# The sixteen largest keys of each block ahead of the guess, and four index searches in banks of their own

## What is computed

```python
x = x + einsum('oc,bchw->bohw', W, layernorm_over_channels(x))   # W: 32 Householder steps
t = tokens(x)                                                     # 16 images x 256 pixels = 4096 tokens of 128
xf = layernorm(t)
Sm = softmax(xf @ W_router + b_router)                            # 4096 x 32 experts
G, idx = top_k(Sm.T, 128)                                         # 128 tokens for each expert
up = tokens_of(idx) @ W_up[group] + b_up                          # 8 groups of 4 experts, 341 wide
y.at[idx].add(G * (silu(up) @ W_down + b_down))
out = t + y
```

## Time and profile before

| what | value |
|---|---|
| median of 3 runs | 203.8 us (203.35 to 204.65) |
| profiled execution, its own time | 202.58 us |
| its span, first to last instruction | 200.3 us |
| mean granted TensorE clock | 0.802 |
| busy share PE, weight load, VectorE, ScalarE, POOL | 64%, 42%, 50%, 40%, 54% |
| instructions | 2418 |

### The profile page before, as it was taken

How to read it: one execution, slowest core, us unless ns; L and a number is a source line. 1 busy time by engine, 2 the same in 40 slices (tenths; PEclk the granted TensorE clock), 3 DMA queues, 4 the chain that set the end, 5 groups by cost and what they waited for, 6 DMA issues and landing times.

```text
span 200.3 us, 2418 instructions
## 1 busy us (share of the span) xinstructions
PE 128.4 (64%) x670; PEld 83.7 (42%) x673; DVE 99.3 (50%) x409; ACT 81.0 (40%) x290; POOL 108.4 (54%) x121
## 2 busy tenths in 40 slices
PE   1999965304116341110126899999999659999992
PEld 1558954201005110000003666666777524444592
DVE  2464998974774882102001021194674962973600
ACT  3265999346992772110134455534334000000062
POOL 2028479986351377777744366866878678300000
PEclk9999999855555555555555699999999969999999
DMA  4999999999755252222220113333424334599167
GB/s 108 298 341 302 292 289 201 305 398 264 190 157 159 88 211 70 63 65 67 65 56 19 49 15 38 29 27 27 40 26 39 29 28 38 101 324 382 63 183 236
DMA packets 33710, 28.45 MB, mean 142 GB/s; under 512 B 6848, under 2 KB 27408, under 8 KB 33568
## 3 DMA queue, kind: packets, MB, share of 16 engines
q1 hardware_dynamic: 26785, 21.70, 37.5%
q0 software_dynamic: 5472, 4.48, 15.3%
q10 hardware_dynamic: 1440, 2.13, 3.3%
HBM read 17.61 MB, written 10.68 MB: 141 GB/s over the span
## 4 chain that ended last, share of the span: by engine, by line
PE 48%; DVE 17%; POOL 12%; issue 10%; another core or an unknown queue 9%; DMA 2%; ACT 1%; SPq 0%; POOLq 0%; DVEq 0%
PE PZ L1184 7%; PE PT L1148 7%; PE PM L1148 6%; PE PZ L1162 6%; POOL rs L472 4%; PE PM L1184 3%; PE PT L1184 3%; PE PM L1162 3%; POOL rs L465 3%; PE PT L992 2%; DVE wdn L935 2%; DVE junk L923 2%; PE PT L1137 2%; POOL act L478 2%
## 5 line engine op out<-in xcount | busy, mean ns | idle before, releaser
L511 POOL DMA_INDIRECT acc<-X,idx x27 | 42.0, 1557 | 18.4 <-DVE X L967 8.0
L502 POOL DMA_INDIRECT xg<-token_rows,idx x32 | 30.4, 949 | 16.3 <-DVE idx L920 8.3
L935 DVE TENSOR_SCALAR_CACHE_REDUCE wdn<-wide,slot_token 128x1024 bf16<-128x1024 f16 x20 | 25.0, 1272 | 5.5 <-PE PZ L1184 5.5
L1125 PE MATMUL PZ<-cum,onehot 32*128 32x129 f16 x32 | 6.7, 265 | 31.3 <-DVE idx L920 18.8
L1040 PE MATMUL PZ<-stage_w,X 128*128 128x192 f32 x64 | 14.7, 381 | 6.9 <-DVE act L767 6.5
L1162 PE MATMUL PZ<-wdn,act 128*128 128x128 f32 x132 | 17.4, 277 | 1.1 <-DVE X L967 1.1
L645 ACT ACTIVATE X<-PZ 128x512 f32<-128x512 f32 x4 | 2.4, 597 | 38.3 <-PE PZ L1189 38.3
L1125 PEld LDWEIGHTS PZ<-cum,onehot 32*128 32x128 f16 x32 | 3.0, 99 | 34.9 <-issue 30.8
L1162 PEld LDWEIGHTS PZ<-wdn,act 128*128 128x128 f32 x132 | 16.0, 191 | 2.1 <-DVE X L967 1.4
L967 DVE TENSOR_SCALAR X<-PZ,xg 128x128 f32<-128x128 f32 x22 | 7.6, 349 | 18.6 <-PE PZ L1162 18.6
L620 ACT ACTIVATE junk_a<-PZ,slot_half 128x128 f16<-128x128 f32 x16 | 5.8, 363 | 26.7 <-issue 20.8
(11 more groups left out here) (180 smaller groups left out, 278.3 us busy)
## 6 DMA issues: line engine op xcount, KB each, us to landing
X<-in_x SPq DMA_DIRECT2D x8, 256.0 KB, 5.2
acc<-zero SPq DMA_DIRECT2D x4, 512.0 KB, 6.3
acc<-x SPq DMA_DIRECT2D x8, 256.0 KB, 5.3
token_rows<-xf SPq DMA_DIRECT2D x8, 256.0 KB, 2.3
xf<-acc ACTq DMA_DIRECT2D x8, 256.0 KB, 5.7
x<-acc SPq DMA_DIRECT2D x8, 256.0 KB, 7.4
out<-X SPq DMA_DIRECT2D x8, 256.0 KB, 2.5
wup<-in_L_ffn_W_up SPq DMA_DIRECT2D x1, 1364.0 KB, 7.8
```

The lines of the kernel that those rows point to most:

```text
L502: nc.gpsimd.indirect_dma_start(out=xg[:, e, :], out_offset=None, in_=rows[:, :], in_offset=bass.IndirectOffsetOnAxis(ap=idx[:, e:e + 1], a ...
L511: nc.gpsimd.indirect_dma_start(out=acc[i][:, :], out_offset=bass.IndirectOffsetOnAxis(ap=idx[:, e:e + 1], axis=0), in_=eo[:, e, :], in_off ...
L935: nc.vector.tensor_scalar(hot(k)[:, r], columns[:, r], slot_token[:, k:k + 1], None, ALU.is_equal, ALU.add, accum_out=found_in[:, k * HOT_ ...
L1125: mm(find_bank(e), onehot[r, g, :], cum[r, g, 0:P + 1], start=True, stop=True).then_inc(s_find, 1)
```

## The change

`leading(0)` moves ahead of `largest(7)`. For each block two functions are new: `without_leading` copies the block with its eight leading keys replaced by 0, `second` takes the eight largest of that. The guess is applied to the 64 leading keys of a partition in one operation, and four maxima over 16 columns give `top8`; its eighth place becomes the larger of itself and the block's sixteenth key. `s_top8` counts one step, no longer four. In the index search experts 0 to 3 read from PZ's banks 2 and 3 and PT's two banks; the second half of the counts is added behind index 1, the second one-hot comes behind index 0, and the wait for these counts moves from search 2 to search 6. Nothing of the check or of the full search is changed.

```diff
-        lead = sb("lead", [P, BLOCKS, 8])
+        lead = sb("lead", [P, BLOCKS, 16])
+        below_guess = sb("below_guess", [P, BLOCKS, 16])
...
         def find_bank(e):
-            return PZ[:, (e + 2) % 4, 0:P + 1]
+            return (PZ[:, 2, 0:P + 1], PZ[:, 3, 0:P + 1], PT[:, 0, 0:P + 1], PT[:, 1, 0:P + 1])[e] if e < 4 else PZ[:, (e + 2) % 4, 0:P + 1]
...
-            pool.wait_ge(s_top8, BLOCKS)
+            pool.wait_ge(s_top8, 1)
             normalise(CH - 2)
...
-                link(nc.vector.max(lead[:, b, :], block(keys2, b)))
+                link(nc.vector.max(lead[:, b, 0:8], block(keys2, b)))
                 nc.vector.tensor_copy(eighth[:, b:b + 1], lead[:, b, 7:8]).then_inc(s_lead, 1)
+
+            def without_leading(b):
+                nc.vector.match_replace(block(upto, b), lead[:, b, 0:8], block(keys2, b), 0.0).then_inc(s_rest, 1)
+
+            def second(b):
+                v.wait_ge(s_rest, b + 1)
+                nc.vector.max(lead[:, b, 8:16], block(upto, b)).then_inc(s_second, 1)
...
+                if g == CH:
+                    leading(0)
                 if 1 <= g <= CH:
                     largest(g - 1)
...
-                    leading(0)
+                    without_leading(0)
                 if g == CH + 2:
+                    second(0)
                     leading(1)
+                    without_leading(1)
...
             leading(2)
+            second(1)
+            without_leading(2)
             leading(3)
+            second(2)
+            without_leading(3)
+            second(3)
...
             v.wait_ge(s_high, 1)
+            v.wait_ge(s_second, BLOCKS)
+            link(nc.vector.scalar_tensor_tensor(below_guess[:, :, :], lead[:, :, :], high[:, 0:1], lead[:, :, :], ALU.is_le, ALU.mult))
             for b in range(BLOCKS):
-                nc.vector.scalar_tensor_tensor(block(upto, b), block(keys2, b), high[:, 0:1], block(keys2, b), ALU.is_le, ALU.mult).then_inc(dch, 1)
-                nch[0] += 1
-            for b in range(BLOCKS):
-                v.wait_ge(dch, nch[0] - BLOCKS + 1 + b)
-                nc.vector.max(top8[:, b, :], block(upto, b)).then_inc(s_top8, 1)
+                ins = nc.vector.max(top8[:, b, :], below_guess[:, b, :])
+            link(ins)
+            nc.vector.tensor_tensor(top8[:, :, 7], top8[:, :, 7], lead[:, :, 15], ALU.max).then_inc(s_top8, 1)
...
             one_hot(0)
-            nc.vector.tensor_tensor(cum[:, GROUPS // 2:, 0:P], PZ[:, 1, :].rearrange("p (g n) -> p g n", n=P),
-                                    base[:, GROUPS // 2:].unsqueeze(2).to_broadcast([P, GROUPS // 2, P]), ALU.add).then_inc(s_cumv, 1)
-            one_hot(1)
             for e in range(E):
                 token_number(e)
+                if e == 0:
+                    one_hot(1)
+                if e == 1:
+                    nc.vector.tensor_tensor(cum[:, GROUPS // 2:, 0:P], PZ[:, 1, :].rearrange("p (g n) -> p g n", n=P),
+                                            base[:, GROUPS // 2:].unsqueeze(2).to_broadcast([P, GROUPS // 2, P]), ALU.add).then_inc(s_cumv, 1)
...
-            pe.wait_ge(s_top8, BLOCKS)
+            pe.wait_ge(s_top8, 1)
...
-                if e == 2:
+                if e == 6:
                     pe.wait_ge(s_cuma, GROUPS // 2)
                     pe.wait_ge(s_cumv, 1)
```

More of the change, by code:

```diff
@@ L294, in metaformer_block @@
         s_cands = sem("candidates_by_expert")
+        s_rest = sem("block_without_its_leading")
+        s_second = sem("second_eight_ready")
         s_high = sem("bracket_ready")
```

## The result

The changed kernel takes 286.32 us (284.85 to 287.93, five runs) where the kernel before takes 203.53 us (202.17 to 204.65, five runs): 1.407 times as long, with an interval of 1.398 to 1.416. The profiled execution took 286.32 us, its span is 284.2 us, 83.9 more than before. The full search runs.

A forecast was written before the change was run, and what follows sets the result against it. VectorE's selection chain, then the index search and PE's experts were taken to bound the kernel. Profiled 202.58 less 1.6 for the shorter path plus 84.2 for the full search gave 285.2, plus 1.2 to the median 286.4 us; range 270 to 312.

The forecast's parts named there:

- The full search runs: At the check after the threshold: four blocks hold 16 or more selected keys, so the 30-round search runs; chance 0.83.
- The first rival: At the flag after the threshold: the selection passes, both gains reach the end, 202.2 us; chance 0.11.
- The price of the search: Between "sel" and PE's transposes of the selection: 84.2 us added, bounds 71 and 102, nothing hiding it.
- seven exponent rounds: In the full search: three small operations, a count and a sum, 2.05 us each, 14.4 us together.
- Twenty-three mantissa rounds: In the full search: four small operations, a count and a sum, 2.22 us each, 51.1 us without loop turns.
- The turn itself: Branch, counter and register waits of the search loop: 0.5 us a turn, 11.5 us together, range 0 to 26.
- The tail: Behind the search rounds: compare, running sum, count, second sum, combination and addition, about 6.2 us, between 5.5 and 8.
- Entry and exit of the search: Entry, flag load and first fill of the full search: 1 us, between 0.2 and 2.
- The selection: From the fourth block's maximum to PE's transpose of the candidates: 0.85 us shorter, bounds 0.3 and 1.4.
- The index order: Ahead of index 0: second half of counts and second one-hot move behind it, 0.75 us gained, bounds 0.5 and 1.2.
- That ends by 65.9, before the first index, so it costs nothing: POOL's dummy gather, moved back about 0.5 us with the row stores, still ends before the first index; cost nothing.
- The second rival: In the index search: the selection passes, but a pair more in the slow stretch costs 3.6 us, 205.8 us; chance 0.06.

The follow-up runs named there:

- noguard: The changed kernel without the maximum that puts a block's sixteenth key in the eighth place; 187.24 us, ratio 0.9987 to the kernel before.
- keys24: The changed kernel with the twenty-four largest keys of each block instead of sixteen, the twenty-fourth in the eighth place; 188.65 us, ratio 1.0064 to the kernel before.

## Why the prediction was right

**The full search runs.** Right, and on the ground that the prediction gave. That the inputs decide was computed, not read from the trace; "noguard" and "keys24" show the same from the chip: without the sixteenth key, or with a limit of 24, the check passes. The count can be redone from the reference's formulas: four blocks, two with 16 and two with 17. The first rival, that the selection passes, is thereby out.

**The price of the search**, 84.2 us forecast, 86.05 measured. By terms: seven exponent rounds 15.0 (14.4 forecast), as a small operation with its wait takes 0.19, not 0.17. Twenty-three mantissa rounds with the loop 63.2 and 0.4 ahead of it (62.6 forecast): a round is 2.75 us. The turn itself is the gap of 0.39 behind L906, where 0.5 was taken; the rest is the small operations again. The Trainium skill, Advanced Engine Details and Errata, Control Flow Timing, has about 108 ns for a compare-and-branch. The row shows 0.39 for the turn of this loop, which also has a counter, a register copy and waits against registers in it, so the figure alone would have been too low. The tail is 7.0 (6.2 forecast): the running sum takes 2.29 us for 1024 columns, where 1.3 was taken. (The pieces that the prediction names for the tail add up to 5.7; the 6.2 stands only with two more small operations and the waits.) Entry and exit of the search are 0.5 together, where 1 was taken.

**The selection**, 0.85 forecast, 0.90 measured, and by the mechanism that was forecast: top8 ready 1.2 us earlier from the fourth block's maximum (1.4 forecast), PE held by the sum of the sign count, which costs 0.3 of it. The replacement over 256 took 0.41 (0.40 forecast), the mask over 64 columns 0.28 (0.20), the four small maxima 0.41 (0.40). **The index order**, 0.75 forecast, 0.69 measured.

**The one step that did not hold** is "That ends by 65.9, before the first index, so it costs nothing". Its shift of 0.5 us was right: in the kernel after the dummy gather comes 0.53 later and ends at 65.67, and index 0 would have been written at about 66.0 to 66.2 without the search. But in "noguard", where it counts, it comes 1.14 later and ends at 66.48, 0.3 us behind index 0. The term that the prediction put at nothing is the landing of the last row store, which takes 0.65 us more there. Under the full search this is hidden, as the first gather is 86 us away. That the 202.2 of the rival would have been reached on the first chip is not shown; on the other chips the 1.5 us at the first gather gave no gain in time that is clear of noise.

**The second rival**, a slow pair more, is not seen: 34.54 us against 34.94 from first gather to experts. The same index, 16, meets the first of the long waits in both traces, though 1.2 us of VectorE's work had moved behind index 0. It begins 7.2 us behind the first gather before and 8.6 after, the index ahead of it at 5.1 and 6.4, so a fixed time of 6.4 to 7.2 us is not excluded; only its price did not show.

Most of the nearness of 286.4 to 286.3 is luck in the sum. The search was put 1.85 us too low. Against that stand the 1.2 us added from the profiled execution to the median, where the profiled execution of the kernel after is its median, and 0.7 us of small differences between the two traces (0.27 ahead at the fourth block, 0.40 less from first gather to experts, and the rest behind). The runs of either kernel spread over 2.5 to 3 us.

## What to carry to other kernels

A guarded shortcut has two prices: its own, and that of its fallback times the chance that the guard fires. Here that was 1.5 us gained at the first gather against 86 us lost, so the first thing to work out is the distribution that the guard tests, on the very inputs: a mean of 8 in 256 reaches 16 in one block of 180, and there are 512 blocks. And before an operation is moved ahead of a broadcast value such as the guess, look at everybody who waits for that value: the sign count gave back 0.3 of the 1.2 us at the transpose, and the stores behind it 0.3 of the 1.8 us at the first gather.

## What the runs showed of the hardware

The kernel before took 203.5 us where it was first measured and 187.8 to 188.2 us on the three chips of the experiments. The traces put it in one place: VectorE's waits between the compare and the next line of the index search, 0.8 to 5.8 us each from 75 us on, with gathers going on at POOL. On the other chips the same waits are 0.04 us with the same gathers beside them, 1.25 us apart, and the last index is there by 79.7 instead of 108.8. So the gathers alone do not make them. What does, the chip, a neighbour on it, or the state of its memory, is open; the stretch did not come back and could not be taken apart. It matters for reading: the same kernel has PE at its end with the stretch, and POOL without it, and an edit's worth depends on which.
